# Between the passes of a four-layer graph network: where the norm's statistics, the layer products and the ELU's minimum are worked out

## The reference

```
h = maximum(layernorm(x), 0);  x = x + L0(h)   # three rounds of "h + mean of the neighbours"
h = maximum(layernorm(x), 0);  x = x + L1(h)   # leaky([h, mean_dst(attr), mean_src(attr)] @ W1 + b1) @ W2 + b2
h = maximum(layernorm(x), 0);  x = x + L2(h)   # attention over the edges
h = maximum(layernorm(x), 0);  x = x + L3(h)   # tensor-product convolution over the edges
L2: x_l = h @ W_l.T + b_l;  x_r = h @ W_r.T + b_r
    e = att . leaky(x_l[src] + x_r[dst]);  alpha = softmax of e over each dst (self loop included)
    out = elu(sum_dst(alpha * x_l[src]) + bias)
```

## Time and profile before

| | |
|---|---|
| median of 3 runs | 2293.53 us (2286.96 to 2294.94) |
| the profiled execution: its own time, its span | 2275.89 us, 2274.1 us |
| busy in the span | PE 1739.4 us (76%), DVE 1806.4 us (79%), ACT 1108.3 us (49%), POOL 859.3 us (38%) |
| TensorE's mean granted clock | 0.767 of 2.4 GHz |
| dense passes | until 912.0 us |
| norm, MLP, norm, x_l and x_r | 912.0 to 977.8 us |
| attention pass | 981.4 to 1640.2 us |
| end of L2, norm, up-projection | 1640.3 to 1690.7 us |
| convolution pass and final update | from 1695.1 us |

### The profile page before, as it was taken

One profiled execution on the slowest core, in us unless ns is written; L12 is line 12 of the kernel. 1 busy time (PEld: TensorE's weight loads), 2 busy tenths in 40 slices (PEclk: granted clock), 3 DMA queues, 4 the chain that ended last, 5 costly groups with the idle time before them and its releaser, 6 DMA issues.

```text
span 2274.1 us, 38102 instructions
## 1 busy us (share of the span) xinstructions
PE 1739.4 (76%) x8653; PEld 1332.9 (59%) x8653; DVE 1806.4 (79%) x5400; ACT 1108.3 (49%) x2824; POOL 859.3 (38%) x861
## 2 busy tenths in 40 slices
PE   2677777998999999645688888788738788878876
PEld 1322224877888887333577778678725555555554
DVE  7988887899899895777777878886387777778775
ACT  0666665887887784210234334334334544444443
POOL 2000000000000000057777777771017777777771
PEclk7755567999999999766587677765557878787888
DMA  4255555765665675055656666652112222222221
GB/s 150 106 152 156 152 150 168 291 229 198 238 242 214 242 260 205 0 163 151 176 162 187 169 167 185 170 168 76 36 40 54 55 54 54 55 55 55 56 56 42
DMA packets 192476, 314.96 MB, mean 139 GB/s; under 512 B 25873, under 2 KB 139416, under 8 KB 182418
## 3 DMA queue, kind: packets, MB, share of 16 engines
q1 hardware_dynamic: 163312, 248.12, 33.4%
q0 software_dynamic: 27712, 63.56, 10.8%
q10 hardware_dynamic: 1250, 0.86, 0.1%
HBM read 232.38 MB, written 80.07 MB: 137 GB/s over the span
## 4 chain that ended last, share of the span: by engine, by line
POOL 24%; PE 19%; issue 12%; DVE 6%; DMA 3%; ACT 1%; DVEq 0%; POOLq 0%; SPq 0%; ACTq 0%
POOL G L682 12%; POOL G L667 8%; POOL SCR L667 4%; PE PS L1881 4%; PE PS L1777 3%; PE PS L1737 3%; PE PS L1987 2%; PE PS L1857 1%; DMA G<-table,src_idx 1%; PE PS L1882 1%; DMA gathered_rows<-G 1%; PE PS L1962 1%; DVE RX L925 1%; ACT HB L699 1%; PE PS L1833 1%
## 5 line engine op out<-in xcount | busy, mean ns | idle before, releaser
L667 POOL DMA_INDIRECT G<-table,src_idx x252 | 264.3, 1049 | 988.7 <-DMA table<-RX 910.4
L682 POOL DMA_INDIRECT G<-table,gather_idx x415 | 408.9, 985 | 277.2 <-DMA table<-RX 151.1
L1987 PE MATMUL PS<-SCR,OH 128*128 128x256 f32 x830 | 284.0, 507 | 109.4 <-DVE SCR L1624 109.2
L1987 PEld LDWEIGHTS PS<-SCR,OH 128*128 128x128 f32 x830 | 203.0, 254 | 162.3 <-DVE SCR L1624 122.0
L1777 PE MATMUL PS<-ALL_R 128*128 128x256 f32 (+3 forms) x2025 | 266.7, 289 | 19.5 <-DVE ALL_R L1216 9.0
L1857 PE MATMUL PS<-RX,OH 128*128 x830 | 187.5, 390 | 120.7 <-DVE SCR L1324 68.6
L1777 PEld LDWEIGHTS PS<-ALL_R 128*128 128x128 f32 (+1 forms) x2025 | 251.5, 191 | 22.5 <-DVE ALL_R L1216 9.4
L1881 PE MATMUL PS<-AT 128*128 128x128 f32 x830 | 252.6, 400 | 15.1 <-issue 7.6
L1857 PEld LDWEIGHTS PS<-RX,OH 128*128 128x128 f32 x830 | 159.0, 271 | 146.0 <-issue 142.7
L830 ACT ACTIVATE AT<-iota,EI 128x128 f32<-128x128 f32 x415 | 132.2, 389 | 194.8 <-PE PS L1882 191.3
L1725 PE MATMUL PS<-AT,G 128*128 128x400 bf16 x474 | 173.4, 495 | 64.2 <-DVE AT L1109 44.8
(11 more groups left out here) (392 smaller groups left out, 3370.8 us busy)
## 6 DMA issues: line engine op xcount, KB each, us to landing
ALL_R<-adjacency SPq DMA_DIRECT2D x72, 1600.0 KB, 6.8
adjacency<-ALL_R SPq DMA_DIRECT2D x26, 1600.0 KB, 7.4
AT<-gathered_rows SPq DMA_DIRECT2D x103, 256.0 KB, 3.7
gathered_rows<-G SPq DMA_DIRECT2D x63, 256.0 KB, 2.7
AT<-dst_in_block SPq DMA_DIRECT2D x103, 128.0 KB, 3.9
gathered_rows<-SCR SPq DMA_DIRECT2D x40, 256.0 KB, 2.3
G<-table,gather_idx POOLq DMA_INDIRECT x415
G<-table,src_idx POOLq DMA_INDIRECT x252
```

The lines of the kernel that those rows point to most:

```text
L667: pool.indirect_dma_start(score_rows(i)[:, q], None, tables[0], bass.IndirectOffsetOnAxis(ap=src_idx[:, v:v + 1], axis=0)).then_inc(s(f"sc ...
L682: pool.indirect_dma_start(G[:, p, q, :], None, tables[i], bass.IndirectOffsetOnAxis(ap=gather_idx[:, p, q:q + 1], axis=0)).then_inc(s(f"{n ...
L1987: ins = pe.matmul(PS[:, q, 0:MSG], OH[:, p, q, :], view(SCR, M_AT + (p * VB + q) * MSG, [[1, MSG]]), start=True, stop=True)
```

## The change

Seven edits, all between the passes but the first:

- In the last layer of the dense passes each block's BN_STATS follows its update, with a wait for its completion; `norm(1)` starts with the aggregation. The statistics lie in `self_score` and `node_max`.
- The product with the means goes first, for five groups before the turning of the blocks, into banks 2 to 6; the turning uses banks 0, 1 and 7, the product with W2 banks 0 and 1.
- x_l and x_r of a block are one product of 256 columns. One flag reports both, and VectorE copies both, each with a bias.
- Biases: b_l + bias goes into x_l, b_r - bias into x_r, and the addition of the bias at the end of L2 goes away.
- The denominators are read in PSUM, without a copy; one product that doesn't need them stands before the wait.
- The ELU's minimum goes to ScalarE: r = relu(-v), then exp(-r), in place of one exponential.
- ScalarE copies out the odd groups of the up-projection.

```
 # norm(n)
+    if n != 1:
+        for b in range(NBLK):
+            ins = dve.bn_stats(node_stats(n, b), X[:, b, :])
+        done(ins)
-    for b in range(NBLK):
-        ins = dve.bn_stats(stats[:, b], X[:, b, :])
-    done(ins)
 # update_node(n), VectorE
     dve.wait_ge(s("block_updated"), u + 1)
+    if i == LAYERS - 1:
+        done(dve.bn_stats(node_stats(1, b), X[:, b, :]))
 # the MLP, TensorE
+    def hidden_of_means(g):
+        w = min(4, NBLK - 4 * g) * P
+        pe.matmul(PS[:, 2 + g % 5, 0:w], w1b_s[:], view(SCR, g * 512, [[1, w]], 32), start=True, stop=False)
+    for g in range(5):
+        hidden_of_means(g)
+    turn_h(0)
     for g in range(7):
+        if g >= 5:
+            pe.wait_ge(s("hidden_biased"), g - 4)
+            hidden_of_means(g)
+        pe.wait_ge(s("ht_ready"), g + 1)
+        pe.matmul(PS[:, 2 + g % 5, 0:w], w1a_s[:], HTF[:, g * 512:g * 512 + w], start=False, stop=True).then_inc(s("hidden_made"), 1)
-        pe.matmul(PS[:, 2 + g % 2, 0:w], w1a_s[:], HTF[:, g * 512:g * 512 + w], start=True, stop=False)
-        pe.matmul(PS[:, 2 + g % 2, 0:w], w1b_s[:], view(SCR, g * 512, [[1, w]], 32), start=False, stop=True).then_inc(s("hidden_made"), 1)
 # x_l and x_r: TensorE, then VectorE after its copy of x_l and its flag for the table
+    ins = pe.matmul(PS[:, 2 * (g % 3) + b // 2, b % 2 * 256:b % 2 * 256 + 256], HTF[:, ...], wlr_s[:], start=True, stop=True)
+    dve.tensor_tensor(XR[:, 4 * g:4 * g + w, :], view(PS, 2 * (g % 3) * 512 + D, [[256, w], [1, D]]),
+                      view(rows_s, 4 * D, [[0, w], [1, D]]), ALU.add).then_inc(s("xr_copied"), 1)
 # the end of L2, VectorE
-    done(dve.tensor_copy(sums8, view(PS, DENS, [[8, NBLK], [1, 8]])))
-    done(dve.tensor_tensor(h_half, h_half, weighted, ALU.add))
-    done(dve.tensor_tensor(h_half, h_half, view(rows_s, 2 * D, [[0, n], [1, D]]), ALU.add))
+    dve.tensor_tensor(h_half, h_half, weighted, ALU.add).then_inc(s("elu_arg"), 1)
-    dve.tensor_scalar(h_half, h_half, 0.0, None, ALU.min).then_inc(s("elu_arg"), 1)
 # the same, ScalarE
-    act.activation(H[:, b0:b1, :], H[:, b0:b1, :], ACT.Exp).then_inc(s("elu_exp"), 1)
+    act.activation(XR[:, b0:b1, :], H[:, b0:b1, :], ACT.Relu, scale=-1.0).then_inc(s("elu_exp"), 1)
+    act.wait_ge(s("elu_exp"), 2 * half + 1)
+    act.activation(XR[:, b0:b1, :], XR[:, b0:b1, :], ACT.Exp, scale=-1.0).then_inc(s("elu_exp"), 1)
```

More of the change, by code:

```diff
@@ L517, in gnn_program @@
         HALVES = ((0, 13), (13, NBLK))
+        turn_bank = lambda n, g: g if n else (0, 1, 7)[g % 3]
         passes = ["score", "conv"]
@@ L813, in _ @@
                 act.wait_ge(s("hidden_made"), g + 1)
-                act.activation(hid[:, g * 512:g * 512 + w], PS[:, 2 + g % 2, 0:w], ACT.Identity, bias=b1_s[:, 0:1]).then_inc(s("hidden_biased"), 1)
+                act.activation(hid[:, g * 512:g * 512 + w], PS[:, 2 + g % 5, 0:w], ACT.Identity, bias=b1_s[:, 0:1]).then_inc(s("hidden_biased"), 1)
             norm_part(2)
[L817 to L820, removed]
             def sum_one_hot(j):
@@ L856, in _ @@
                 act.wait_ge(s("elu_arg"), half + 1)
-                act.activation(H[:, b0:b1, :], H[:, b0:b1, :], ACT.Exp).then_inc(s("elu_exp"), 1)
+                act.activation(XR[:, b0:b1, :], H[:, b0:b1, :], ACT.Relu, scale=-1.0).then_inc(s("elu_exp"), 1)
+                act.wait_ge(s("elu_exp"), 2 * half + 1)
+                act.activation(XR[:, b0:b1, :], XR[:, b0:b1, :], ACT.Exp, scale=-1.0).then_inc(s("elu_exp"), 1)
             norm_part(3)
+            for g in range(1, 7, 2):
+                act.wait_ge(s("up_made"), g + 1)
+                act.activation(view(RX, XL_AT + g * 512, [[1, 4 * P]]), PS[:, g, :], ACT.Copy, scale=32.0 ** -0.5).then_inc(s("up_copied_act"), 1)
             def conv(k, p, m):
@@ L1259, in _ @@
             row = lambda i: rows_s[:, i * D:(i + 1) * D]
-            dve.tensor_tensor(row(3), row(3), row(4), ALU.add)
-            dve.tensor_tensor(row(2), row(2), row(4), ALU.subtract)
+            dve.tensor_tensor(row(3), row(3), row(2), ALU.add)
+            dve.tensor_tensor(row(4), row(4), row(2), ALU.subtract)
             done(dve.tensor_tensor(X[:], X[:], view(rows_s, 0, [[0, NBLK], [1, D]]), ALU.add))
@@ L1527, in _ @@
             done(dve.tensor_tensor(node_max[:], old, node_max[:], ALU.mult))
-            for b0, b1 in HALVES:
+            for half, (b0, b1) in enumerate(HALVES):
                 n = b1 - b0
@@ L1664, in turn_h @@
                     if b % 4 == 0:
+                        if n == 0 and b >= 12:
+                            pe.wait_ge(s("ht_ready"), b // 4 - 2)
                         if b < 4 * ACT_GROUPS:
@@ L1668, in turn_h @@
                             pe.wait_ge(s("normed_dve"), n + 2)
-                    ins = pe.transpose(PS[:, b // 4, (b % 4) * P:(b % 4 + 1) * P], H[:, b, :], ident[:])
+                    ins = pe.transpose(PS[:, turn_bank(n, b // 4), (b % 4) * P:(b % 4 + 1) * P], H[:, b, :], ident[:])
                     if b % 4 == 3 or b == NBLK - 1:
@@ L1819, in _ @@
                 for b in range(w):
-                    ins = pe.matmul(PS[:, 4 + g % 2, b * P:(b + 1) * P], hid[:, (4 * g + b) * P:(4 * g + b + 1) * P], w2_s[:], start=True, stop=True)
+                    ins = pe.matmul(PS[:, g % 2, b * P:(b + 1) * P], hid[:, (4 * g + b) * P:(4 * g + b + 1) * P], w2_s[:], start=True, stop=True)
                 ins.then_inc(s("mlp_made"), 1)
@@ L1830, in _ @@
                     pe.wait_ge(s("xr_copied"), g - 2)
-                for side in range(2):
-                    for b in range(min(4, NBLK - 4 * g)):
-                        ins = pe.matmul(PS[:, 2 * (g % 3) + side, b * P:(b + 1) * P], HTF[:, (4 * g + b) * P:(4 * g + b + 1) * P],
-                                        wlr_s[:, side * P:(side + 1) * P], start=True, stop=True)
-                    ins.then_inc(s("xr_made" if side else "xl_made"), 1)
+                for b in range(min(4, NBLK - 4 * g)):
+                    ins = pe.matmul(PS[:, 2 * (g % 3) + b // 2, b % 2 * 256:b % 2 * 256 + 256], HTF[:, (4 * g + b) * P:(4 * g + b + 1) * P],
+                                    wlr_s[:], start=True, stop=True)
+                ins.then_inc(s("xlr_made"), 1)
             def spread_ends():
```

41 lines of the change are left out of this document (22 added, 19 removed).

## The result

The changed kernel takes 2275.67 us (median of 14 runs, 2262.64 to 2285.42), the kernel before 2286.26 (14 runs, 2275.90 to 2295.38). The ratio is 0.9951, its 95% interval 0.9932 to 0.9969: 11 us faster, between 7 and 15.5. The forecast was 14.4 us faster, and 2279.

The account below looks back on a forecast made before the run. TensorE was taken to bound the last dense layer, VectorE right behind; elsewhere each stage's chain decides. Terms summed to −14.4 us: 2261.5 for an execution like the profiled one, 2279 against the 2293.53 median, range 2267 to 2291.

Parts of the forecast that it names:

- Statistics out of the norm, into the layer: Norm and last dense layer: 25 statistics leave the norm, −4.65 us; 0.32 each in the layer costs +2.7.
- The +0.3 for the means: Last dense layer, step 74: the means, on the path, queue behind a statistic's wait, +0.3 us.
- The first rival: Last dense layer: statistics only change places, at 0.45 a step costing +5 to +6 us; 2282, chance 0.16.
- a price of 0.20: Last dense layer: a statistic costs 0.20 us a step, as in the norm, making the layer's term +0.9.
- The clock: MLP: early products in TensorE's idle time keep full clock for the turning and first product, −1.7 us together.
- Means' products first: MLP: five products of 1.06 us leave the stretch behind the turning and hide in the norm, −5.3 us.
- x_l and x_r: Products for x_l and x_r: about no change in TensorE's products, a tail of VectorE copies, +0.6 us.
- The +5 for loads: Products for x_l and x_r: upper bound if each of the 50 weight loads shows by 0.1 us.
- End of L2: End of L2: VectorE instructions go, ScalarE's extra ones hidden by some 0.5 us; −6.2 us, −3.5 without the cover.
- The prediction's own last sign: Attention pass: lasts its 659 us; a difference above 5 us either way would make the prediction wrong.
- the third rival: Attention pass: earlier start shifts it against the clock, +15 us per 20 us window that falls; slower, chance 0.05.
- the second rival: MLP and x_l/x_r: products don't get cheaper, clock falls and loads show; 2286, no change, chance 0.21.

Follow-up runs that it names:

- b_late_stats: Changed kernel with 18 blocks' statistics taken after the last batches and the ELU's minimum back on VectorE; first aggregation at 139.0 us of the stretch instead of 142.0.
- d_warm128: Changed kernel with means' products paired behind the turning, ahead of the features', and four idle 128-row products before it; aggregation to W2 products 23.3 us against 19.7.
- after_third: The changed kernel, unchanged, timed again in another session; median 2272.99 us (12 runs), ratio 0.9948 to the kernel before.
- c: Changed kernel with the turning first, then seven pairs of products, the means' ahead of the features' in each; the pairs took 25.4 us.
- g: Changed kernel with the turning first, then seven pairs of products, the features' ahead of the means' in each; the pairs took 13.7 us.
- h_warm_close: Changed kernel with statistics behind the batches' end, plus 11 and 10 idle 128-row products before the second and third norms' turnings; 2266.35 us, ratio 0.9927.

## Why the prediction was nearly right

- **Statistics out of the norm, into the layer.** The price (0.34 against 0.32), the bound (VectorE in the steps with two batches) and the waits came as described: three, the longest 1.0 us, 2.1 together where 3 were forecast. The batches' steps got 2.7 us longer, as forecast, and from the last step to the first aggregation the change takes 5.8 us instead of 10.4, the 4.65 of the forecast. The +0.3 for the means isn't seen. The sum of the part is −2.0 (−1.65 forecast). The first rival (5 to 6 us in the layer) is out, and so is a price of 0.20: with that, by the prediction's own count, the layer would have lost 0.9. In b_late_stats two statistics with no wait behind them take 897.11 − 896.71 = 0.40 us, 0.20 each; with a wait behind each it is 0.34. The Trainium skill ("VectorE: DVE Perf Modes", "The DRAIN you can't avoid") has the semaphore cost nothing extra, measured on eight copies in a row. These traces, of statistics, disagree by 0.14 us each.
- **The clock.** The step that failed is "With five products in that idle time I take the full clock for the turning", worth −1.7. The clock fell to 0.50 in all nine traces with the early products. d_warm128, with products of 128 rows in their place, held 1.00, so the 32 rows are the likely cause. The early products took 6.8, 6.7 and 6.4 us in the three traces instead of 5.3, and the turning, all or most of it at half clock, ended 12.5, 12.4 and 11.1 us after the aggregation instead of 11.5. The first product with the features was at most 0.3 us slow, in before 0.5 in one trace and not at all in the other, so what that gained is the execution's draw as much as the change's. Together the clock's term came to about +0.4 (an estimate: 0.5 from the turning's end, −0.1 from the first product). The prediction had named this case, with a bound of +3. The Trainium skill ("TensorE: Matmul & The Clock Gate", "What's actually happening") sets the clock by how busy the engine has been. The traces agree where the work is of 128 rows; with 32 rows TensorE was busy for 4.00 of 4 us and lost the clock.
- **Means' products first.** −5.3 was forecast, about −6.2 came: the products behind the turning take 7.2 us at full clock (after_third) and 13.4 in pairs (d_warm128). The prediction carried 1.06 us over to each product. But in pairs each product follows one with other weights, and starts are 1.05 us apart; the five with the features stand in a row, on the same weights, and start 0.86 apart. So two errors partly cancel: from the aggregation to the W2 products it went from 25.2 us (24.8 in the second trace) to 19.7 (19.7 in the second, 18.1 in the third, where the clock was back early in the turning), −5.8 on average, where −7.0 was forecast. The prediction also missed what another order risks: in the one execution with the means' product right behind the turning, the MLP took 11.6 us longer.
- **x_l and x_r.** +0.6 was forecast for the tail with no change in the products. At equal clock about +0.7 came (12.5 against an estimated 11.7); the products themselves got 0.3 to 0.4 shorter, so the tail is about 1.1. The +5 for loads didn't come.
- **End of L2.** −6.2 forecast, −6.2 measured, hidden by 0.6 us where 0.5 was expected.
- **Up-projection.** −0.2 between first and last flag, as forecast.
- **The attention pass.** The prediction's own last sign, that a difference of more than 5 us there would make it wrong, did come: 662 and 678 us before, 677, 685 and 680 after. The sign was badly chosen, since the unchanged kernel alone differs by 16 us between two executions.
- **From 14 to 11.** The edited stages lost 14.0 us, the medians 11. The interval, 7 to 15.5, holds both, so it need not mean anything. What speaks for a part given back is the attention pass: in the five traces of kernels without early means' products (before twice, c, d, g) it started at 976 us or later and took 662 to 678 us, 669 on average; in the nine with them it started at 966 to 973 and took 673 to 685, 678 on average. The stretch of full clock in the last sums, worth 6 us, is in four of the five and in none of the nine. That is the mechanism of the third rival at a fraction of its size. Taken at their word, these 9 us would leave 5 of the 14, less than the interval allows, so the traces overstate it. Whether the early start, the order in the MLP or chance decides it stays open: no run moved the start of the pass alone.
- **The level, and a slip.** That the changed kernel's 2275.67 lies near the forecast 2279 is in part luck: the forecast stood on a median of 2293.53 from three runs, and over 14 the kernel before takes 2286.26. In the second rival, half of 4.7 and half of 4.4 make −9.9, not −8.

## What to carry to other kernels

A few instructions moved into a pass whose engines are all near their limit cost what the tightest steps have too little; read each step's slack, and put them where the waiting engine waits (here behind the last batch). In a wait of TensorE, useful work of 32 rows filled the time here but didn't hold the clock. It was worth its place all the same: 19.7 us against 23.3 with idle products of 128 rows. Put products on the same weights in a row, and behind a phase at half clock let the product of 128 rows come first, as far as one run of each order shows it. And compare stages from their own starts: here one profiled pair showed 1.3 us where 14 had been gained in the edited stages.

## What the runs showed of the hardware that was not expected

- Products with 32 rows of weights at 4.00 of 4 us busy: the granted clock fell from 1.00 to 0.50 within 916 to 920 us, and so in all nine traces with them; four products of 128 rows in the same place held 1.00 (one trace).
- Pairs of a 32-row and a 128-row product, TensorE never idle: at 0.50 for 25 us where the 32-row product came first behind the turning (one trace), at 1.00 from within the first product where it came second (three traces). Entered at 1.00, pairs with the 32-row product first held it (d_warm128).
- Products of 512 columns start 0.86 us apart on the same weights and 1.05 apart where the weights alternate, both at full clock.
- The same turning got the clock back 3.1 us after its start in one execution of the changed kernel and 5.7 us after it in another.
- Turning in two groups of four and then 17 without a break (a group 0.66 us of work, then 0.88 us of waiting) held 1.00 in d_warm128 and lost it in h_warm_close, at the same pace.
- The last scores to the end of the attention pass, the same instructions in 14 traces: 90 us in four, 96 in ten, with no length between.
